# Routed-expert loops of a fused layer: the five steps of a tile spread over seven turns instead of five, with another order of steps in a turn

## The reference

```python
def ffn(x, gate_w, gate_b, w1_s, w2_s, w3_s, w1_r, w2_r, w3_r):      # 16 experts, inner width 176
    scores = sigmoid(einsum('ed,btd->bte', gate_w, x)) + gate_b
    weights, indices = top_k(scores, 4)
    weights = weights / weights.sum(-1, keepdims=True)
    shared = silu(x @ w1_s) * (x @ w3_s) @ w2_s
    h3 = silu(einsum('btd,edc->btec', x, w1_r) * einsum('btd,edc->btec', x, w3_r))
    routed = sum over a token's four experts of  weight * (h3[expert] @ w2_r[expert])
    return shared + routed

x = x + 0.5 * ffn(layernorm(x), ...)
x = x + scan_layer(layernorm(x), ...)
x = x + 0.5 * ffn(layernorm(x), ...)      # the same weights again
```

## Time and profile before

| what | us |
|---|---|
| time, median of 3 runs (588.7 to 592.06) | 591.58 |
| span of the profiled execution, first to last instruction | 644.2 |
| of it, stretch of the first routed loop (81 to 262) | 181 |
| of it, stretch of the second routed loop (407 to 592) | 185 |

### The profile page before, as it was taken

The page is one execution under the profiler, slowest core; times in us unless marked ns, Lnnn a source line. Parts: engine busy times, 40 slices in busy tenths (PEclk is TensorE's granted clock), DMA queues, the critical chain, the costliest instruction groups (busy, mean ns, idle before and its releaser), DMA issues.

```text
span 644.2 us, 13458 instructions
## 1 busy us (share of the span) xinstructions
PE 517.4 (80%) x3206; PEld 454.5 (71%) x3207; DVE 434.0 (67%) x1459; ACT 376.0 (58%) x1128; POOL 349.6 (54%) x364
## 2 busy tenths in 40 slices
PE   4976799999999999667586943799999899998460
PEld 3954589998888889455465931599988788887350
DVE  6798667767767677527686689467666667666434
ACT  2778466766657567555474664477766666665010
POOL 3899554456556565465311442544565556655764
PEclk9978589999999999697697975599999999999875
DMA  9971245565444445432100560254444454555644
GB/s 297 391 269 68 60 130 156 163 179 153 151 145 135 147 129 138 126 95 79 53 2 0 167 210 0 66 150 133 132 150 131 132 149 130 145 137 142 190 129 121
DMA packets 61149, 88.24 MB, mean 137 GB/s; under 512 B 9499, under 2 KB 46363, under 8 KB 61107
## 3 DMA queue, kind: packets, MB, share of 16 engines
q1 hardware_dynamic: 47379, 50.29, 22.7%
q0 software_dynamic: 13728, 37.50, 22.6%
HBM read 57.22 MB, written 30.54 MB: 136 GB/s over the span
## 4 chain that ended last, share of the span: by engine, by line
PE 56%; DVE 11%; issue 10%; ACT 9%; POOL 5%; another core or an unknown queue 4%; DMA 4%; SPq 1%; ACTq 0%; POOLq 0%; DVEq 0%
PE bank L1380 24%; PE bank L1431 10%; PE bank L1402 6%; POOL mamba_room L595 5%; PE bank L1442 4%; PE bank L1441 4%; PE bank L1599 2%; DMA ys_scratch<-ring_f 2%; PE bank L1488 2%; ACT ring_f L713 1%; ACT ring_r L664 1%; DVE xres L1159 1%; PE bank L1624 1%; PE bank L1453 1%
## 5 line engine op out<-in xcount | busy, mean ns | idle before, releaser
L560 POOL DMA_INDIRECT ring_f<-xn_scratch,tokidx x158 | 149.6, 947 | 153.0 <-PE bank L1402 100.6
L1380 PE MATMUL bank<-w_routed,ring_r 128*128 x948 | 195.5, 342 | 0.9 <-DVE ring_r L954 0.8
L1380 PEld LDWEIGHTS bank<-w_routed,ring_r 128*128 128x128 f32 x948 | 152.2, 192 | 6.6 <-issue 4.1
L1431 PE MATMUL bank<-w_routed,ring_r 128*128 x790 | 119.5, 281 | 3.0 <-ACT ring_f L692 2.1
L1431 PEld LDWEIGHTS bank<-w_routed,ring_r 128*128 128x128 f32 x790 | 110.0, 188 | 4.3 <-issue 4.3
L673 ACT ACTIVATE ring_r<-bank 128x256 fp32r<-128x256 f32 x158 | 60.7, 384 | 71.4 <-PE bank L1442 66.5
L962 DVE TENSOR_TENSOR ring_r<-bank,ring_r 128x128 fp32r<-128x128 f32 x158 | 45.6, 288 | 59.9 <-ACT ring_r L673 47.4
L595 POOL DMA_INDIRECT mamba_room<-ys_scratch,si x64 | 61.6, 962 | 29.1 <-issue 18.4
L954 DVE TENSOR_TENSOR ring_r<-bank,ring_r 128x256 fp32r<-128x256 f32 x158 | 67.1, 425 | 15.1 <-issue 5.4
L1402 PE MATMUL bank<-cst,ring_f 128*128 128x128 f32 x316 | 64.4, 286 | 10.0 <-DMA ring_f<-xn_scratch,tokidx 5.4
L682 ACT ACTIVATE stage<-bank 128x176 f32<-128x176 f32 x158 | 50.6, 320 | 35.7 <-remote 18.2
(11 more groups left out here) (172 smaller groups left out, 816.5 us busy)
## 6 DMA issues: line engine op xcount, KB each, us to landing
ys_scratch<-ring_f SPq DMA_DIRECT2D x158, 128.0 KB
raw_routed<-in_w13r SPq DMA_DIRECT2D x6, 704.0 KB, 12.5
xn_scratch<-w_routed SPq DMA_DIRECT2D x32, 128.0 KB, 4.9
raw_routed<-in_w2r SPq DMA_DIRECT2D x6, 512.0 KB, 12.8
raw_routed<-in_w13r SPq DMA_DIRECT2D x8, 352.0 KB, 6.4
ring_f<-xn_scratch,tokidx POOLq DMA_INDIRECT x158
xres<-in_x_in SPq DMA_DIRECT2D x4, 512.0 KB, 6.4
raw_routed<-in_w2r SPq DMA_DIRECT2D x8, 256.0 KB, 6.7
```

Source lines behind the costliest of these rows:

```text
L560: pool.indirect_dma_start(xg[j % UN], None, xn_dram, bass.IndirectOffsetOnAxis(ap=tokidx[:, j:j + 1], axis=0)).then_inc(s_g[j % UN], 16)
L1380: last = pe.matmul(out, a, b, start=(q == 0), stop=(q == len(terms) - 1))
L1431: last = pe.matmul(p_y[b][:, 0:D], a, v, start=(q == 0), stop=(q == 4))
```

## The change

The lags of the routed loop become 0 (x), 2 (up-projection), 4 (turn of `hid`) and 6 (down-projection), where they were 0, 1, 2 and 4. The order of an engine's steps in a turn changes with them: PE goes hidden, ht, x, out (before: x, hidden, out, ht); ACT goes first, slot_out, x, silu, ht (before: first, ht, x, silu, slot_out); DVE goes product, x, early rows, ht (before: product, early rows, ht, x). Steps of ACT and DVE that stood one turn behind the PE step that they follow now stand in the same turn.

Waits that the old order made needless are now made in every turn: `pe_hidden` for the product two slots back, `pe_ht` for the low part two slots back; the wait for the turn two slots back moves from `act_first` to `dve_product`. As the register group of a slot's expert number must now live for seven turns, there are three groups of four, and PE's loop body is 12 turns. `EARLY_FIRST` and `TABLE_AFTER` move by two, with the down-projection. No instruction of the computation is added or removed.

```diff
-LAG_X, LAG_H, LAG_T, LAG_Y = 0, 1, 2, 4
-PE_UN = 2 * UN
+LAG_X, LAG_H, LAG_T, LAG_Y = 0, 2, 4, 6
+EXPERT_GROUPS = 3
+PE_UN = EXPERT_GROUPS * UN
...
-EARLY_FIRST, EARLY_ADD = 29, 3
+EARLY_FIRST, EARLY_ADD = 31, 3
...
-TABLE_AFTER = 76
+TABLE_AFTER = 74
...
 act_first:     act.wait_ge(s_h, base + n + 1)
-                    if f == 1 or not (isinstance(i, int) and c < 2):
-                        act.wait_ge(s_ht, f * NS + n - 1)
...
-                pipeline(act, NS, [(LAG_H + 1, act_first(f, base)), (LAG_T + 1, act_ht(f)), (LAG_X, act_x(base)),
-                                   (LAG_H + 1, act_silu(base)), (LAG_Y + 1, act_slot_out(f)), (LAG_Y + 1, act_roots(f))],
+                pipeline(act, NS, [(LAG_H, act_first(f, base)), (LAG_Y + 1, act_slot_out(f)), (LAG_X, act_x(base)),
+                                   (LAG_H, act_silu(base)), (LAG_T, act_ht(f)), (LAG_Y + 1, act_roots(f))],
...
-            def dve_product(base):
+            def dve_product(f, base):
                     dve.wait_ge(s_a, base + i * UN + c + 1)
+                    if f == 1 or not (isinstance(i, int) and c < 2):
+                        dve.wait_ge(s_ht, f * NS + i * UN + c - 1)
...
-                pipeline(dve, NS, [(LAG_H + 1, dve_product(base)), (LAG_T + 1, add_early(f)), (LAG_T + 1, dve_ht(f)),
-                                   (LAG_X, dve_x(base)), (LAG_X, shared_rows_first(f)), (LAG_X, measure_early(f))],
+                pipeline(dve, NS, [(LAG_H, dve_product(f, base)), (LAG_X, dve_x(base)), (LAG_T, add_early(f)),
+                                   (LAG_T, dve_ht(f)), (LAG_X, shared_rows_first(f)), (LAG_X, measure_early(f))],
...
 pe_hidden:     pe.wait_ge(s_xlo, n + 1)
-                    if isinstance(i, int) and c < 2:
-                        pe.wait_ge(s_m, n - 1)
+                    pe.wait_ge(s_m, n - 1)
...
 pe_ht:         pe.wait_ge(s_s, f * NS + i * PE_UN + c + 1)
-                    if f == 1 and isinstance(i, int) and c < 2:
-                        pe.wait_ge(s_hlo, NS + c - 1)
+                    if f == 1 or not (isinstance(i, int) and c < 2):
+                        pe.wait_ge(s_hlo, f * NS + i * PE_UN + c - 1)
...
-                pipeline(pe, NS, [(LAG_X, pe_experts), (LAG_X, pe_x(f, base)), (LAG_H, pe_hidden(base)),
-                                  (LAG_Y, pe_out(f)), (LAG_T, pe_ht(f, base))], PE_UN)
+                pipeline(pe, NS, [(LAG_X, pe_experts), (LAG_H, pe_hidden(base)), (LAG_T, pe_ht(f, base)),
+                                  (LAG_X, pe_x(f, base)), (LAG_Y, pe_out(f))], PE_UN)
```

More of the change, by code:

```diff
@@ L1103, in stage @@
                     for n in range(EARLY):
-                        if early_step(n) == c + LAG_T + 1:
+                        if early_step(n) == c + LAG_T:
                             row_added(f, n)
@@ L1278, in _ @@
                 for n in range(EARLY):
-                    if early_step(n) >= NS + LAG_T + 1:
+                    if early_step(n) >= NS + LAG_T:
                         row_added(f, n)
@@ L1381, in mm3 @@
                 return last
-            e_reg = [[pe.alloc_register(f"expert{g}_{k}") for k in range(UN)] for g in range(2)]
+            e_reg = [[pe.alloc_register(f"expert{g}_{k}") for k in range(UN)] for g in range(EXPERT_GROUPS)]
             def pe_experts(i, c):
                 if c % UN == 0:
-                    pe.reg_load(e_reg[c // UN % 2], te[0:1, ds(i * PE_UN + c, UN)])
+                    pe.reg_load(e_reg[c // UN % EXPERT_GROUPS], te[0:1, ds(i * PE_UN + c, UN)])
             def routed_weights(c):
-                e = pe.snap(e_reg[c // UN % 2][c % UN], min_val=0, max_val=NE - 1)
+                e = pe.snap(e_reg[c // UN % EXPERT_GROUPS][c % UN], min_val=0, max_val=NE - 1)
                 return lambda rows, h, a, m: w_routed[0:rows, ds(e, 1), h, a:a + m]
```

## The result

| kernel | median of the timed runs | ratio to before, 95% interval | profiled execution: time, span |
|---|---|---|---|
| before | 590.67 us (4 runs) | 1 | 644.2 us span in the profile that stood ahead |
| after | 596.53 us (4 runs, 595.37 to 598.49) | 1.0098 (1.0066 to 1.0130) | 598.49 us, 596.5 us |

A forecast was written before the change was run, and what follows sets the result against it. PE's issue was taken to bound the routed loops at 2.0 us a turn. 591.6 - 1.8 (late signals) + 0.4 (loop ends) + 0.3 (table load) = 590.5 us; own range 586 to 596, widened to 572 to 597.

The forecast's parts named there:

- the second rival: Routed loops: DVE and ACT form a chain longer than a turn, 0.1 us a turn, 607 us; chance 0.15.
- PE's floor of 2.0 us a turn: Routed loops: PE's own work takes 1.99 us a turn, and no order of the steps changes it.
- Timed runs don't have the late signals: PE's signals reach ACT and POOL 0.4 to 1.55 us late in the profile; timed runs mostly lack this.
- The first rival: Late signals are real in timed runs too and the change covers them: around 575 us, full gain 557; chance 0.27.
- the span after would be near 620: Profile of the kernel after: span near 620 us while the timed runs stay near 590.
- the third rival: POOL's 4.61 us cycle for two turns holds, so no profile gain; time as forecast, sharing its chance of 0.58.
- -1.8 us of gain: Routed loops, timed runs: a twentieth taken of the 35.5 us that covering late signals could give.
- The slack: Routed loops after: 1.6 us between x and up-projection, 2.0 us between up-projection and ht, over the latest signal's 1.55.
- The ends of the loops, 0.2 us each, bound 1: Filling and draining gain two turns but the same instructions: 0 to 1 us a loop, 0.2 taken.
- The table load: Round 0: table load and two activations now ahead of the last ht, 0 to 1.7 us, 0.3 taken.
- The eighth fetch: Fetches after gather 78 become eight instead of seven: 0 to 1 us, taken as nothing.

The follow-up runs named there:

- a_lag4: The kernel after with the old lags 0, 1, 2, 4, EARLY_FIRST 29 and TABLE_AFTER moved along; 713.69 us, 1.2091 to before.
- b_again: The kernel before, unchanged, run and profiled once more; 589.05 us, ratio 0.9996.
- a_early29: The kernel after with EARLY_FIRST back at 29, so seven early fetches behind the last gather instead of eight; 595.22 us, 1.0089 to before.
- a_htfirst: The kernel after with one swap, ScalarE's ht ahead of the silu of its turn; 592.72 us, 1.0033 to before.
- a_noload: The kernel after with TensorE's expert registers loaded only at each loop's first turn; 595.32 us, 1.0073 to before.
- a_outlast: The kernel after with ScalarE's output of a slot put back to the end of its turn; 628.17 us, 1.0644 to before.

## Why the prediction was wrong

The measured 596.5 us lies just inside the end of the range, 597, which was put there for the second rival, and outside the forecast's own 586 to 596; that the range reached so far is no merit of the forecast's mechanism.

*PE's floor of 2.0 us a turn*: right, for both kernels. That no order of the steps changes it held only while the lags cover the order; a_lag4 with 2.8 us a turn shows the bound of that sentence.

*Timed runs don't have the late signals*: right, and the most useful step. b_again has a span of 590.8 us for the same program, and 51 turns in 100 us where the disturbed profile had 2.35 us a turn. The first rival falls with it. The rule that it cited from the Trainium skill, Runtime: NRT & Kernel Launch, section "The ~15µs preamble/postamble breakdown", has the profile's total about 6.2 us over the time: the trace does not agree, as in after's execution the span, first to last instruction, lies 2.0 us under the time. What stretched the one execution to 644.2 us stays open. That the span after would be near 620 was wrong, since that execution was not disturbed at all; whether the lags would cover late signals, and so the third rival, stays untried.

*-1.8 us of gain*: there was nothing to give back, 0.

*The slack*: this is the step that failed. The sum rested on each chain alone, x to up-projection and up-projection to ht, and TensorE's waits in the drain are on neither (between up-projection and ht it left out the ht of the turn, 0.22 us; the slack is larger still). What it left out is the chain across slots that the new order of ScalarE's turn closes: silu, ht, low part, product, silu. The second rival had seen it ("ACT's ht, which ACT now runs last in its turn") and counted 1.9 to 2.3 us; measured are 1.83 us, and 2.28 with a shared row. Early rows, which it had in the count, lie in DVE's wait for ht and cost nothing (239.07 to 239.54 in the round of 1.83 us above). Where it went wrong is the sentence against it, that a slack of 1.6 us lets a long turn be made up in the next: a turn gives back 2.0 - 1.83 = 0.17 us. So the rival came true in part, not as 0.1 us on each turn, but as a few long turns behind the shared rows and late writes and as the drain: 3.8 us by the swap, of the 15.8 that it was priced at.

*The ends of the loops, 0.2 us each, bound 1*: mis-sized. First x to the end of the last down-projection is 1.6 and 2.5 us more than before, in part in the drain, whose last steps wait on the ring. That the ends "wait on chains that the lags don't lengthen" left the order of ScalarE's steps out. *The table load*: TensorE's last two down-projections wait 0.98 us for the output of slot 75, which the load holds back; this is inside its bound, and moving the load gave nothing that the runs could tell. *The eighth fetch*: taken as nothing, and a_early29 against after, 1.0089 and 1.0098, is not told from that.

**Open**: what a_htfirst still lacks, 0.33% (0.03 to 0.64). With four buffers it is 0.39%, with intervals that overlap. In those profiles TensorE ends 10.0 and 9.5 us behind the last x, against 7.2 and 7.2 in b_yb4, but its last x comes 1.5 and 2.3 us sooner, and in a_htfirst both loops together are 1.3 us shorter than in b_again (330.9 and 332.2). So the deeper drain is a candidate that these profiles do not bear out, and the cause of the rest stays open.

**The version that beats both** is b_yb4: the order and lags of before, four output buffers, 584.22 us, 1.1% under before.

## What to carry to other kernels

When an order puts two engines' steps of different slots behind each other, write down the ring that it closes, add up one round with the extra work that some turns have, and compare it with the bound engine's turn: the difference is all that makes up a delay, whatever slack each chain has by itself. A group whose idle time goes to another engine's line, while that engine's idle time goes back to the first (30.2 and 35.4 us here), is the sign to look for such a ring; where its round is shorter than the bound engine's turn, it costs only what a delay in it cannot make up. Before a forecast rests on a profile that is 9% over the timed runs, expect the undisturbed execution and ask what of the argument is left.

## What was not expected of the hardware

An output buffer's write, 128 KB, held ScalarE up to 2.52 us within a loop (after, at 536.94) though each turn is 2.0 us and two buffers give a turn in between. Four buffers were worth 1.0 to 1.1% in three kernels. What makes a write late is not shown: of the 14 waits in b_again, two (1.59 us at 107.46, 1.34 us at 403.19) come before the first early row of their loop is fetched, at 133.57 and 431.16; the twelve others cluster at the ends of the loops, from 226.83 and from 518.54 on, and none lies between 134 and 226, where a row is fetched about every 4 us.

TensorE's load of four registers every fourth turn costs nothing that the runs can tell in after (a_noload 1.0073 against 1.0098, intervals that overlap), and some 17 us in a_outlast, where ScalarE's output stands last in its turn (628.17 us, and 611.48 without the loads).
